# A transformer kernel on one core: TensorE multiplies constants at the beginning of four phases, and the first phase begins with its own loads

## The reference, cut to what matters

```python
x = x + _L0_xattn_ref(_layernorm(x), ctx, ...)         # attention over the context, 16 heads of 8
x = x + _L0_ffn_ref(_layernorm(x), Wr, Wqkv, Wo)       # each of 8 experts chooses 8 tokens of a sequence
x = x + _L1_xattn_ref(_layernorm(x), ctx, masks, ...)  # self attention, cross attention, relu layer
x = x + _L1_ffn_ref(_layernorm(x), ...)                # 16 routed experts and 2 shared ones
```

## Time and profile before

| | us |
|---|---|
| median of 3 runs | 2242.87 |
| lowest and highest | 2231.62, 2249.71 |
| the profiled execution | 2243.04 |
| its span | 2241.2 |
| PE busy | 2013.2 (90%) |
| DVE busy | 1674.5 (75%) |
| mean granted clock | 0.96 |

### The profile page before, as it was taken

The page is one execution under the profiler, slowest core; times in us unless marked ns, Lnnn a source line. Parts: engine busy times, 40 slices in busy tenths (PEclk is TensorE's granted clock), DMA queues, the critical chain, the costliest instruction groups (busy, mean ns, idle before and its releaser), DMA issues. The chain is left out here.

```text
span 2241.2 us, 53213 instructions
## 1 busy us (share of the span) xinstructions
PE 2013.2 (90%) x19268; PEld 1559.0 (70%) x19268; DVE 1674.5 (75%) x4618; ACT 1062.6 (47%) x2084; POOL 449.3 (20%) x504
## 2 busy tenths in 40 slices
PE   5999995687768999996999997995999999999998
PEld 3666664566655666664666665774888888888887
DVE  3777775877744888886888886665888888888786
ACT  3666662455544555553555553443444444443443
POOL 0111110000001322322122222563111111121111
PEclk9999997999987999997999998997999999999999
DMA  3000000000000000001001001000000000000000
GB/s 112 30 28 28 28 9 1 1 1 0 0 1 1 1 0 0 0 0 29 28 20 28 28 19 48 16 0 0 6 6 10 5 5 10 5 5 10 5 5 10
DMA packets 27255, 30.37 MB, mean 14 GB/s; under 512 B 1936, under 2 KB 20624, under 8 KB 26896
## 3 DMA queue, kind: packets, MB, share of 16 engines
q1 hardware_dynamic: 27152, 29.18, 4.2%
HBM read 24.98 MB, written 4.19 MB: 13 GB/s over the span
## 5 line engine op out<-in xcount | busy, mean ns | idle before, releaser
L429 DVE TENSOR_REDUCE mx<-ps 128x8 f32<-128x512 f32 x384 | 262.3, 683 | 180.7 <-PE ps L574 180.3
L338 ACT ACTIVATE ex<-ps 128x512 f32<-128x512 f32 x384 | 230.5, 600 | 269.9 <-PE ps L592 268.1
L1097 ACT ACTIVATE moe_sg<-ps 128x512 f32<-128x512 f32 x288 | 172.9, 600 | 356.8 <-PE ps L1149 356.6
L1133 PEld LDWEIGHTS ps<-down,moe_act 128*128 128x128 f32 x2048 | 267.2, 191 | 22.3 <-DVE moe_acc L1341 1.4
L592 PE MATMUL ps<-pack,sh 128*128 128x128 f32 x1536 | 252.6, 287 | 32.0 <-DVE sh L431 31.3
L431 DVE TENSOR_TENSOR sh<-ps,mx 128x512 f32<-128x512 f32 x384 | 265.5, 691 | 13.2
L1133 PE MATMUL ps<-down,moe_act 128*128 128x128 f32 x2048 | 269.7, 275 | 0.4 <-DVE moe_acc L1341 0.4
L1323 DVE TENSOR_TENSOR moe_act<-ps,moe_sg 128x512 f32<-128x512 f32 x288 | 198.2, 688 | 84.9 <-PE ps L1149 70.7
L608 PEld LDWEIGHTS ps<-vblk,ex 128*64 128x64 f32 x6144 | 214.3, 140 | 65.6 <-issue 65.6
L592 PEld LDWEIGHTS ps<-pack,sh 128*128 128x128 f32 x1536 | 170.3, 143 | 126.7 <-issue 66.2
L608 PE MATMUL ps<-vblk,ex 128*64 128x32 f32 x6144 | 257.3, 227 | 0.0
(11 more groups left out here) (237 smaller groups left out, 3443.5 us busy)
## 6 DMA issues: line engine op xcount, KB each, us to landing
ctxT<-in_ctx SPq DMA_DIRECT2D x32, 256.0 KB, 2.9
x_res<-in_x SPq DMA_DIRECT2D x16, 256.0 KB, 2.9
kmi<-in_key_mask SPq DMA_DIRECT2D x16, 256.0 KB, 3.4
out<-moe_acc SPq DMA_DIRECT2D x16, 256.0 KB, 2.3
pack<-in_pack SPq DMA_DIRECT2D x1, 2440.5 KB, 8.8
wqkv<-in_wqkv SPq DMA_DIRECT2D x1, 1536.0 KB, 8.3
gate<-in_gate SPq DMA_DIRECT2D x6, 192.0 KB, 4.0
up<-in_up SPq DMA_DIRECT2D x6, 192.0 KB, 4.1
```

Of the source, the lines that this page charges most:

```text
L338: nc.scalar.activation(ex[:, u % 2], UB[u % 4].rearrange("p (c n) -> p c n", n=P), ACT.Exp).then_inc(e_ready, 1)
L429: nc.vector.tensor_reduce(mx[:, u % 2], sc, AX.X, ALU.max).then_inc(max_done, 1)
L1133: last = nc.tensor.matmul(YB[k % 2][:, t * D:(t + 1) * D], act_[:, k % 3, t * P:(t + 1) * P], down[:, k, :], start=True, stop=True)
```

## The change

Five things, all in the program's text:

1. A new helper `stay_busy` lets PE multiply the first 128 columns of `pack` with its first 512, n times over, into a bank that nobody reads before it is written anew. It stands ahead of the first real instruction of PE in the phases a=1 (n = 18), a=2 (15), experts (20) and choice (16), and once more in the choice phase behind the logits (12). It waits for nothing.
2. `setup_phase` goes. Its constants are made in the phase a=0: four fills ahead of that of `vblk`, two small ones as soon as the first part of `pack` is there, the rest at the end of the first step on DVE.
3. `pack` is laid out anew, so that its first 775 columns are what a=0 needs (`a0`, `ident`, `headmask`), and comes in two transfers, with the first loads of `x` and the context between them.
4. The two small products for `qscale` run in the last step of a=0, the copy behind them too.
5. PE, ACT and POOL wait in a=0 for what the setup phase had made before them.

```diff
-for _n, _w in [("a0", ATTN_W), ("a1", ATTN_W), ("a2", ATTN_W), ("ident", P), ("headmask", 4),
+for _n, _w in [("a0", ATTN_W), ("ident", P), ("headmask", 4), ("a1", ATTN_W), ("a2", ATTN_W),
...
             if cross:
+                if a == 0:
+                    sp.dma_start(pk[:, 0:FIRST], setup["pack_in"][:, 0:FIRST]).then_inc(pack_loaded, 16)
                 loads(0, 0)
                 loads(1, 1)
+                if a == 0:
+                    sp.dma_start(pk[:, FIRST:PACK], setup["pack_in"][:, FIRST:PACK]).then_inc(rest_loaded, 16)
+                    for r in range(4):
+                        sp.dma_start(setup["qmi"][32 * r:32 * r + 32, :, :],
+                                     setup["q_mask"].rearrange("(f r) k -> r f k", f=2)).then_inc(qmask_loaded, 16)
...
+                if a == 0 and first:
+                    later_constants()
...
+            if a == 0:
+                first_constants()
             nc.vector.memset(vblk[:, :, :, :, :], 0.0).then_inc(vblk_set, 1)
...
+            if a == 0:
+                loaded_constants()
             pipelined(dve, NG, prep, step)
...
             def prep(g, s):
+                if a == 0:
+                    pe.wait_ge(pack_loaded, 16)
+                else:
+                    stay_busy(nc, UB[0], pk, 18 if a == 1 else 15)
                 for v in range(UNITS):
                     prep_slot(g, s, v, True)
...
+                    if a == 0 and not more and v == 2:
+
+                        pe.wait_ge(qscale_diag, 2)
+                        for f in (0, 1):
+                            last = nc.tensor.matmul(PREP[:, 0:S], setup["ones"][0:32, :], setup["diag"][0:32, f, :],
+                                                    start=f == 0, stop=f == 1)
+                        last.then_inc(qscale_ready, 1)
...
+def stay_busy(nc, bank, pack, n):
+
+    for _ in range(n):
+        nc.tensor.matmul(bank, pack[:, 0:P], pack[:, 0:512], start=True, stop=True)
...
             def prep(g, s):
+                stay_busy(nc, GB_[0], C["pack"], 20)
                 make_xT(g, s)
                 logits(g, s)
...
             def prep(g, s):
+                stay_busy(nc, bank(5), C["pack"], 16)
                 make_xT(g, s)
                 make_logits(g, s)
+                stay_busy(nc, bank(5), C["pack"], 12)
                 make_token_rows(g, s)
...
-        setup_phase(nc, ps, C, pack_in, q_mask, pack, work)
```

More of the change, by code:

```diff
@@ L64, with attention_phase @@
 HQ = 4
-def attention_phase(nc, ps, C, x_res, y_res, x_in, ctx_in, key_mask, a, ahead=()):
+def attention_phase(nc, ps, C, x_res, y_res, x_in, ctx_in, key_mask, a, ahead=(), setup=None):
     cross = a != 1
@@ L476, in normalise, with first_constants, loaded_constants, later_constants @@
                 last.then_inc(z_done, 1)
+            def first_constants():
+                nc.vector.memset(C["mhalf"][:, :], -0.5)
+                nc.vector.memset(C["half"][:, :], 0.5)
+                nc.vector.memset(C["oneb"][:, :], 1.0 / 32)
+                nc.vector.memset(setup["ones"][:, :], 1.0).then_inc(consts_set, 1)
+            def loaded_constants():
+                dve.wait_ge(pack_loaded, 16)
+                bias = COLS["a0"][0] + 5 * D
+                nc.vector.tensor_scalar(C["bkm"][:, 0, :], headmask, pk[:, bias + 1:bias + 2], None, ALU.mult
+                                        ).then_inc(consts_set, 1)
+                nc.vector.tensor_scalar(C["bqs"][:, :], pk[:, bias:bias + 1], SCALE, None, ALU.mult
+                                        ).then_inc(consts_set, 1)
+            def later_constants():
+                dve.wait_ge(rest_loaded, 16)
+                for n in (1, 2):
+                    bias = COLS[f"a{n}"][0] + 5 * D
+                    nc.vector.tensor_scalar(C["bkm"][:, n, :], headmask, pk[:, bias + 1:bias + 2], None, ALU.mult
+                                            ).then_inc(later_set, 1)
+                nc.vector.tensor_copy(C["identb"].rearrange("p f k -> p (f k)"), C["ident4"]).then_inc(later_set, 1)
+                dve.wait_ge(qmask_loaded, 64)
+                nc.vector.tensor_scalar(C["qmask"], setup["qmi"][:, :, :], 0.0, NEG, ALU.is_equal, ALU.mult
+                                        ).then_inc(qbias_done, 1)
+                dve.wait_ge(qbias_done, 1)
+                nc.vector.tensor_reduce(setup["any"][:, 0:2], C["qmask"], AX.X, ALU.max).then_inc(qany_done, 1)
+                dve.wait_ge(qany_done, 1)
+                nc.vector.tensor_scalar(setup["any"][:, 2:4], setup["any"][:, 0:2], 0.0, SCALE, ALU.is_equal, ALU.mult
+                                        ).then_inc(qany_done, 1)
+                dve.wait_ge(qany_done, 2)
+                for f in (0, 1):
+                    nc.vector.tensor_scalar(setup["diag"][:, f, :], C["ident4"][:, S * f:S * f + S],
+                                            setup["any"][:, 2 + f:3 + f], None, ALU.mult).then_inc(qscale_diag, 1)
             def prep(g, s):
@@ L504, in step @@
                             normalise(g - 1, 1)
+                    if a == 0 and not more and v == 5:
+                        dve.wait_ge(qscale_ready, 1)
+                        nc.vector.tensor_copy(C["qscale"][:, :], PREP[:, 0:S]).then_inc(qscale_copied, 1)
+                if a == 0 and first:
+                    later_constants()
                 if not more:
@@ L1924, in _ @@
             pipelined(dve, N, prep, step)
[L1927 to L1984, removed]
@@ L2005, in build @@
         C["qscale"] = sb("qscale", [P, S])
-        work = {"qmi": sb("qmi", [P, 2, S], I32), "ones": sb("ones", [P, P]), "any": sb("qany", [P, 4]),
+        setup = {"pack_in": pack_in, "q_mask": q_mask, "qmi": sb("qmi", [P, 2, S], I32), "ones": sb("ones", [P, P]), "any": sb("qany", [P, 4]),
                 "diag": sb("qdiag", [P, 2, S])}
-        setup_phase(nc, ps, C, pack_in, q_mask, pack, work)
         with ExitStack() as early:
```

20 lines of the change are left out of this document (19 added, 1 removed).

## The result

The changed kernel takes 2261.17 us (median of 11 runs, 2254.61 to 2265.55), the kernel before 2242.89 us in the same series (11 runs, 2231.62 to 2249.99). The ratio is 1.008, 95% interval 1.0062 to 1.0099: slower, by 18 us, and less than 1%. The forecast was 2264 us, with 2246 to 2279 as its range.

The account below looks back on a forecast made before the run. PE was taken as the bound, busy 90% of the span, with its clock lost at phase borders. Terms -11.0 + 4.3 + 3.7 + 9.9 + 14.5 = +21.4 us on 2243.04 gave 2264.4 us, range 2246 to 2279.

Parts of the forecast that it names:

- The price of a product: In all batches, instructions follow each other every 0.43 us; a product is two, 0.86 us at the full clock.
- rival 2: Products cost half, 0.43 us each, so choice and a=1 are covered by idle time: 2228 us; chance 0.08.
- The cold start: A batch beginning at the low clock costs 2 us extra, bounds 0 and 4; half of that in choice.
- a=0: -11.0: Phase a=0 gets 11.0 us shorter as earlier loads let PE begin sooner; bounds -8 to -12.
- The cover that I named for the moved constants: At the end of a=0's step 0, 1.7 us of constants hide in 3.37 us in which DVE waits for PE.
- Choice: +4.3: Choice gets 4.3 us longer: its batches delay PE by 6.8 us, warm work gives back 2.5; bounds +2 to +7.
- a=1: +3.7: Phase a=1 gets 3.7 us longer: 6.3 us delay, 2.6 regained, and step 0 as cold as today.
- rival 1: The clock stays up in a=1, making step 0 8 us shorter: 2254 us, 2251 if a=2 keeps it also; chance 0.17.
- a=2: +9.9: Phase a=2 gets 9.9 us longer: the batch delays PE by 12.0 us, 2.1 come back; bounds +7 and +13.
- what the warm clock gives back: In a=2, the first warm product, the transposes and half of a later line save 2.1 us before the clock falls.
- Step 0 was almost all warm already: In a=2, step 0 takes 18.25 us before the change, so a warm clock has nothing left to gain there.
- Experts: +14.5: The experts phase gets 14.5 us longer: 15.0 us delay, only 0.5 regained in the transposes; bounds +13 and +17.

Follow-up runs that it names:

- e1: The changed kernel without any of the five batches, the new start of a=0 kept; first series: 2234.49 us, ratio 0.9988 to the kernel before.
- e1b: The changed kernel without any of the five batches, run again in the third series beside the changed kernel: 2228.92 us, ratio 0.9941 to the kernel before.
- b1_before: The kernel before, with no edit, profiled a second time in a single execution: 2243.29 us.
- b2_before: The kernel before, with no edit, profiled a third time in a single execution: 2249.87 us.
- e1c_no_batches: The changed kernel without any of the five batches, one more single profiled execution: 2234.26 us.
- e3: The changed kernel without the batch of 20 in the experts phase, the other four batches kept: 2242.74 us, ratio 1.0025 to the kernel before.
- e5: The changed kernel with batches cut to PE's idle time, plus 3 products in a=1's pause ahead of the value projection: 2221.12 us, ratio 0.9933 to the kernel before.
- e6: As e5, plus 3 products in a=0 while PE waits for ACT's normalised tokens: 2218.19 us, ratio 0.9895 to the kernel before.
- e8: As e6, plus 2 products in a=2 while PE waits for ACT's key copy: 2219.53 us, ratio 0.9893 to the kernel before.

## Why the prediction was right

**The price of a product** was right: 36 instructions in 15.69 us are (15.69 - 0.59) / 35 = 0.43 us each. The Trainium skill's figure of about 131 ns for a sustained stream ("TensorE: Matmul & The Clock Gate", Back-to-back issue gap) is not seen in these float32 products either, and with it rival 2 is out. The cold start was 2 us in the forecast. With 0.43 us between instructions, a=2's batch has 16.12 - 0.59 - 29 x 0.43 = 3.1 us more than a warm one, that of the experts phase 20.15 - 0.59 - 39 x 0.43 = 2.8. The first batch of the choice phase (32 instructions in 15.67 us) has 1.8 more, where I had put 0.9.

**a=0: -11.0, measured -11.2** in three pairs with the same rise of the clock. The cover that I named for the moved constants is there only when the clock is low; with an early rise the next maximum starts right behind them. Between the first maximum and the end the three pairs lose 0.3 to 0.7 us. I had reckoned 0.4, for the two small products of `qscale`; whether it is these or the moved constants, the runs don't tell.

**Choice: +4.3, measured +3.5. a=1: +3.7, measured +2.8.** Both as foretold in kind: the delay, the few warm instructions, and in a=1 the clock that falls ahead of step 0, against rival 1. In choice two sizes were off and cancelled: the transposes of the chosen places came 7.5 us later instead of 6.8, and what is behind them gave back 3.4 us instead of 2.5 (the phase is 4.1 us longer between the two profiles). In a=1 the first maximum is 2.6 to 3.2 us later in the four profiles with the batch of 18, and the clock is back 43.0 us into the phase in three of them and 44.9 in the changed kernel; without it, 43.0 in five of six and 40.7 in one.

**a=2: +9.9, measured +8.7** by the means, and that closeness is luck. At the first maximum the changed kernel is 12.0 us later, and 12.7 at the end of relu, near the upper bound of 13. Two terms were too small or too large: the cold start (3.1 us, not 2), and what the warm clock gives back (1.06 us, L608 alone, not 2.1). The mean is lower because of the other side: "Step 0 was almost all warm already" was true of three of the six profiles without batches (before, e1, e1b: the clock is back 20 us into the phase), while in b1_before, b2_before and e1c_no_batches it came back after 34, 34 and 42 us.

**Experts: +14.5, measured +15.6**, and by e3 16: the cold start was 1 us too small.

**The sum: +21.4, measured +18.** The terms by the profiles give 30.6 - 11.2 = +19.4. What I did not have is that a profile of the kernel before is one draw: 2243 us were the median by good luck, with an a=0 at the slow end and an a=2 at the fast one. That a change under 1% cannot be told from none here was wrong: with 11 runs of each the interval, 1.0062 to 1.0099, leaves out 1.

**Open.** In the first series the kernel without batches stood at 0.9988, in the third at 0.9941, and the intervals do not meet. There, 14 of 33 runs of the kernel before lay between 2229.8 and 2231.9 us, which none of 23 on the other chip in the second and third series did. Whether the moments of the clock's changes depend on the chip or the series, I cannot tell from these runs. Also open is what in step 0 of a=1 lets the clock fall; e5 shows only that it isn't the pause ahead of it. So is what makes it fall early near the end of a=2 in e5, e6 and e8.

## What to carry to other kernels

Work that keeps an engine warm must fit, in its real duration, into the idle time that the trace shows ahead of the first real operand: here a float32 product of 512 columns costs 0.86 us, and batches of 10 to 17 us stood in gaps of 3 to 9. Batches that did fit paid, even though the clock fell again some us later: the first maximum came 3 us earlier in a=0 (e6, e8), 4.6 in a=1 (10 + 3 products) and 3.4 in a=2 (1 + 2), and the choice phase was 4.9 us shorter. What they saved is the float32 work of PE on the chain right behind them. Where that chain has next to none, as in the experts phase, nothing is to be had (717.4 to 717.8 us with 2 products as without). And where one kernel's phases differ by 9 to 11 us from one execution to the next, compare phases at the same event, not totals of single profiles.

## What the runs showed of the hardware

- The time of one program depends on when the granted clock rises in the first steps of an attention phase: the same a=0 ends between 335.2 and 344.1 us (eight profiles), a=2 with relu takes 478.4 to 489.9 us (the six without batches), while the experts phase repeats within 0.7 us (717.1 to 717.8 without its batch of 20).
- A busy PE is not a warm PE. In step 0 of a=1 of the changed kernel it is busy 5.00 of 5 us from 685 to 690 us at a clock of 0.50, while the clock came up during eight float32 instructions (four products) of 512 columns on all 128 rows. In step 0 most products use 32 rows (the scores) or move 32 columns (the weighted sums); whether that is the reason was not tested.
- Near the end of a=2 the clock was low for 44 us in three profiles (e5_fill_a1, e6_fill_a0, e8_fill_a2; from 1327.7 us in e6), in steps that ran warm in the eleven others, where it was low for 14 to 21 us.
- A product that fills a pause of PE ahead of the first maximum can raise the clock for the chain up to there and not for the step behind it: in e8_fill_a2 the transposes of a=0 take 0.66 us at 23.93 us and 1.12 us at 25.41.
